# The first batch's attention input made inside the second batch's mixer stages instead of in a stage of its own

## The reference

```
x = _layernorm(x + _L0_attn_ref(x, ...))   # mixer: RMS norm, projections, convolution, state scan, gate
x = _layernorm(x + _L0_ffn_ref(x, ...))    # 4-bit block quantisation, 128x128 product
x = _layernorm(x + _L1_attn_ref(x, ...))   # attention, 16 heads of 64
x = _layernorm(x + _L1_ffn_ref(x, ...))    # experts: 8 routed, top 2, and a shared one
```

```
mu = jnp.mean(latents, axis=-1, keepdims=True)
var = jnp.mean((latents - mu) ** 2, axis=-1, keepdims=True)
x = (latents - mu) * jax.lax.rsqrt(var + 1e-05) * ln_gamma + ln_beta
q = (x @ Wq)...; k = (x @ Wk)...; v = (x @ Wv)...
```

## Time and profile before

| | us |
|---|---|
| median of 3 runs | 3421.25 |
| lowest and highest | 3419.8, 3422.25 |
| the profiled execution | 3422.55 |
| its span in the profile | 3420.8 |

### The profile page before, as it was taken

The page is one execution under the profiler, slowest core; times in us unless marked ns, Lnnn a source line. Parts: engine busy times, 40 slices in busy tenths (PEclk is TensorE's granted clock), DMA queues, the critical chain, the costliest instruction groups (busy, mean ns, idle before and its releaser), DMA issues. The chain is left out here.

```text
span 3420.8 us, 57281 instructions
## 1 busy us (share of the span) xinstructions
PE 3228.0 (94%) x20859; PEld 1947.6 (57%) x20861; DVE 2327.9 (68%) x3746; ACT 1999.1 (58%) x3828; POOL 2707.2 (79%) x1342
## 2 busy tenths in 40 slices
PE   6995899399999999999999999999999999998998
PEld 2554455155555555555555555555555555554898
DVE  3887688666667666666666776666676666664664
ACT  6984797245555555555655665555555555554454
POOL 1881386079999999999999999999999999996333
PEclk9997899699999999999999999999999999999999
DMA  2220121210000000000000000000000000000000
GB/s 51 91 87 21 53 89 59 59 28 1 4 1 4 4 1 4 1 4 1 4 1 4 7 7 7 1 4 1 4 1 4 4 1 2 1 1 22 20 24 12
DMA packets 66053, 59.95 MB, mean 18 GB/s; under 512 B 7786, under 2 KB 49332, under 8 KB 65716
## 3 DMA queue, kind: packets, MB, share of 16 engines
q1 hardware_dynamic: 63970, 55.93, 5.6%
q10 hardware_dynamic: 1810, 0.37, 0.1%
HBM read 49.46 MB, written 6.82 MB: 16 GB/s over the span
## 5 line engine op out<-in xcount | busy, mean ns | idle before, releaser
L1610 POOL TENSOR_TENSOR den_g<-den_g,p 128x1024 f32<-128x1024 f32 x888 | 2116.7, 2384 | 142.7 <-ACT p L1532 24.9
L1685 DVE TENSOR_REDUCE quarters<-psum 128x1 f32<-128x512 f32 x2004 | 1291.4, 686 | 648.8 <-PE psum L1061 604.4
L1532 ACT ACTIVATE p<-psum 128x512 f32<-128x512 f32 x2048 | 1084.4, 600 | 384.8 <-PE psum L1409 337.1
L1422 PE MATMUL psum<-p,v 128*64 128x512 f32 x4096 | 922.8, 592 | 0.0
L1422 PEld LDWEIGHTS psum<-p,v 128*64 128x64 f32 x4096 | 293.3, 137 | 582.0 <-issue 506.9
L1061 PE MATMUL psum<-k_main,q_main 64*128 64x512 f32 x2048 | 449.4, 424 | 6.9 <-DVE quarters L1068 5.6
L652 POOL TENSOR_TENSOR fed_s<-dx,work 128x1024 f32<-128x1024 f32 x128 | 302.2, 2363 | 179.2 <-POOLq L593 160.6
L1409 PE MATMUL psum<-row_shift,row_ones 64*128 64x512 f32 x2048 | 415.8, 389 | 0.0
L1409 PE MATMUL psum<-q_main,k_main 64*128 64x512 f32 x2048 | 413.4, 391 | 2.2 <-PEq L1201 2.2
L1409 PE MATMUL psum<-q_main,k_rest 64*128 64x512 f32 x2048 | 415.1, 390 | 0.0
L1409 PE MATMUL psum<-q_rest,k_main 64*128 64x512 f32 x2048 | 414.7, 390 | 0.0
(11 more groups left out here) (284 smaller groups left out, 3233.3 us busy)
## 6 DMA issues: line engine op xcount, KB each, us to landing
work<-bc_rows SPq DMA_DIRECT2D x128, 256.0 KB, 3.1
resid<-in_resid SPq DMA_DIRECT2D x8, 256.0 KB, 4.2
x_mid<-resid SPq DMA_DIRECT2D x8, 256.0 KB, 2.6
residual<-x_mid SPq DMA_DIRECT2D x8, 256.0 KB, 4.7
x<-x_mid SPq DMA_DIRECT2D x8, 256.0 KB, 2.8
out<-mixed SPq DMA_DIRECT2D x8, 256.0 KB, 2.3
xa<-x_mid SPq DMA_DIRECT2D x4, 256.0 KB, 3.6
w_qkv<-in_Wq SPq DMA_DIRECT2D x16, 64.0 KB, 1.9
```

Source lines behind the costliest of these rows:

```text
L1422: last = nc.tensor.matmul(o_bank[hi(h), :], vv[:, kt, hi(h)], p[:, u % LIVE, h, :], start=(kt == 0), stop=(kt == KT - 1))
L1532: nc.scalar.activation(p[:, u % LIVE, h, :], bank_of["score", u, h], ACT.Exp, scale=float(DH) ** -0.5).then_inc(p_ready, 1)
L1610: nc.gpsimd.tensor_tensor(sums, first, src, ALU.add).then_inc(added_g, 1)
L1685: nc.vector.reduce_max(quarters[:, to % 2, h, n:n + 1], bank_of["max", u, h], X_AXIS).then_inc(max_read, 1)
```

## The change

The block `attention_input` goes. Its steps are made from `resids[0]`, the mixer's buffer, while the second batch's mixer runs:

- in the second batch's `mixer_inputs`, VectorE makes the 16 statistics and aggregates behind its passes over PSUM, and GpSimd makes roots and offsets (`norm_roots`, with the power on GpSimd) into `stat_in`, which gets a fourth row;
- in the second batch's `mixer_output`, ScalarE scales the 16 tiles into `scaled_in` behind its half of the first norm, TensorE turns them into banks 4 to 7 behind the bias products, and ScalarE writes them to `xaT0` with gamma and beta. TensorE waits for `in_taken` before it turns the quantised values into the same banks. SP loads gamma, beta and the six weights of the first pairs at the head of this block;
- `xaT0`, `gamma`, `beta` and `w_qkv` are allocated ahead of phase 1; `xaT` becomes a list of two tiles;
- the set-up block has no DMA any more, and Wo's two loads go to the head of SP's queue in `attention_first`.

The diff, cut to its core:

```diff
+def norm_roots(nc, pool, st, two, stat, exponents, ready):
+    var, y, t, offset = (stat[:, i, :] for i in range(4))
+    pool.wait_ge(ready, TILES)
+    st.link(nc.gpsimd.tensor_scalar(var, two[:, :, 1], EPS, None, ALU.add))
+    st.link(nc.gpsimd.tensor_tensor(y, var, exponents, ALU.pow))
+    st.link(nc.gpsimd.tensor_tensor(t, y, y, ALU.mult))
+    st.link(nc.gpsimd.tensor_tensor(t, t, var, ALU.mult))
+    st.link(nc.gpsimd.tensor_scalar(t, t, -0.5, 1.5, ALU.mult, ALU.add))
+    st.link(nc.gpsimd.tensor_tensor(y, y, t, ALU.mult))
+    st.link(nc.gpsimd.tensor_tensor(offset, two[:, :, 0], y, ALU.mult))
+    return nc.gpsimd.tensor_scalar(offset, offset, -1.0, None, ALU.mult)
...
# mixer_inputs
+        else:
+            @block.gpsimd
+            def _(pool):
+                st = Steps(pool, pool_step)
+                norm_roots(nc, pool, st, two, stat_in, exponents[:], averaged).then_inc(roots, 1)
+                pool.wait_ge(roots, 1)
...
+            if following is None:
+                for t in range(TILES):
+                    nc.vector.bn_stats(six[:, t, :], resids[0][:, t, :]).then_inc(measured, 1)
+                dve.wait_ge(measured, TILES)
+                for t in range(TILES):
+                    nc.vector.bn_aggr(two[:, t, :], six[:, t, :]).then_inc(averaged, 1)
...
# mixer_output, TensorE
+                if last_batch:
+                    turn_input(nc, pe, psum, 4, scaled_in, ident, in_scaled, in_turned)
                 pe.wait_ge(quantised, 1)
                 for c in range(CHUNKS):
-                    if b + 1 < BATCH:
-                        pe.wait_ge(in_taken, c + 1)
+                    pe.wait_ge(in_taken, c + 1)
...
# mixer_output, SyncE
+                if last_batch:
+                    sp.dma_start(gamma[:], ins["ln_gamma"]).then_inc(weights, 16)
+                    sp.dma_start(beta[:], ins["ln_beta"]).then_inc(weights, 16)
+                    for pair in range(2):
+                        for i, w in enumerate(("Wq", "Wk", "Wv")):
+                            sp.dma_start(w_qkv[:, pair, i, :], ins[w][:, pair * P:(pair + 1) * P]).then_inc(weights, 16)
...
# mixer_output, ScalarE
+                    if turn == 1 and last_batch:
+                        for t in range(TILES):
+                            nc.scalar.activation(scaled_in[:, t, :], resids[0][:, t, :], ACT.Identity, scale=stat_in[:, 1, t:t + 1],
+                                                 bias=stat_in[:, 3, t:t + 1]).then_inc(in_scaled, 1)
+                        act.wait_ge(weights, 16 * 8)
+                        for c in range(CHUNKS):
+                            act.wait_ge(in_turned, c + 1)
+                            nc.scalar.activation(xaT0[:, piece(c)], banks(psum, 4 + c), ACT.Identity, scale=gamma[:, 0:1],
+                                                 bias=beta[:, 0:1]).then_inc(in_taken, 1)
...
# phase2
-                @block.sync
-                def _(sp):
-                    sp.dma_start(gamma[:], ins["ln_gamma"]).then_inc(loaded, 16)
-                    sp.dma_start(beta[:], ins["ln_beta"]).then_inc(loaded, 16)
-                    sp.wait_ge(loaded, 32)
...
-        attention_input(nc, ins, x_in, 0, common)
-        attention_first(nc, 0, common, experts)
+        attention_first(nc, ins, 0, common, experts)
...
# attention_first, SyncE
+                    for pair in range(2):
+                        sp.dma_start(w_o[:, pair, :], ins["Wo"][pair * P:(pair + 1) * P, :]).then_inc(w_o_loaded, 16)
                     for dst, src in experts["loads"]:
                         sp.dma_start(dst, src).then_inc(experts["loaded"], 16)
+                    sp.wait_ge(w_o_loaded, 32)
```

More of the change, by code:

```diff
@@ L214, in build @@
         shared = dict(ident=ident, ident_bf=ident_bf, ones=ones, exponent=exponent, psum=psum)
-        phase1(nc, ins, x_mid[0], **shared)
+        first = dict(xaT0=ph.sbuf("xaT0", [P, SEQ]), gamma=ph.sbuf("gamma", [P, 1]), beta=ph.sbuf("beta", [P, 1]),
+                     w_qkv=ph.sbuf("w_qkv", [P, 2, 3, P]))
+        phase1(nc, ins, x_mid[0], first, **shared)
         with Phase(nc) as late:
@@ L218, in build @@
             tail = attention_tail(late)
-            phase2(nc, ins, x_mid[0], x_mid[1], experts, tail, **shared)
+            phase2(nc, ins, x_mid[0], x_mid[1], experts, tail, first, **shared)
             phase3(nc, ins, x_mid[0], x_mid[1], out, experts, tail, **shared)
@@ L450, in mixer_inputs @@
         big = su.sbuf("big", [P, len(units), PIECE])
-        loaded, step, pool_step, squares, roots, in_scaled = (
-            su.sem(s) for s in "loaded step pool_step squares roots in_scaled".split())
+        loaded, step, pool_step, squares, roots, in_scaled, measured, averaged = (
+            su.sem(s) for s in "loaded step pool_step squares roots in_scaled measured averaged".split())
         conv_psum, conv_done, in_psum, tapped, tap_silu, skip_psum, skip_done = (
@@ L800, in mixer_scan, with mixer_output @@
         nc.all_engine_barrier(sems_to_clear=sem_range(su.sems))
-def mixer_output(nc, x_out, b, m):
+def mixer_output(nc, ins, x_out, b, m):
     resid, work, xnT, scaled_in, norm_w, ident, stat, gain_act, ffn_parts, bias_parts, ones_bf, psum, ident_bf, six, two = (
         m[k] for k in "resid work xnT scaled_in norm_w ident stat gain_act ffn_parts bias_parts ones_bf psum ident_bf six two".split())
+    resids, stat_in = m["resids"], m["stat_in"]
+    xaT0, gamma, beta, w_qkv = (m["first"][k] for k in "xaT0 gamma beta w_qkv".split())
+    last_batch = b + 1 == BATCH
     with Phase(nc, f"_o{b}") as su:
@@ L896, in attention_tail, with phase2 @@
         residual=ph.sbuf("residual", [P, CHUNKS, TPC, D]))
-def phase2(nc, ins, x_in, x_out, experts, tail, ident, ident_bf, ones, exponent, psum):
+def phase2(nc, ins, x_in, x_out, experts, tail, first, ident, ident_bf, ones, exponent, psum):
     with Phase(nc) as ph:
[L903 to L909, removed]
+        gamma, beta, w_qkv = (first[k] for k in "gamma beta w_qkv".split())
+        xaT = [first["xaT0"], ph.sbuf("xaT1", [P, SEQ])]
         v = ph.sbuf("v", [P, 2, TILES, P])
@@ L924, in phase2 @@
         shift = ph.sbuf("shift", [P, 2 * TPC, 64], BF16)
-        common = {k: x for k, x in locals().items() if k not in ("nc", "x_in", "x_out", "ins", "ph", "experts", "tail")}
+        common = {k: x for k, x in locals().items() if k not in ("nc", "x_in", "x_out", "ins", "ph", "experts", "tail", "first")}
         common.update(tail)
@@ L1275, in attention_pairs @@
     o_raw, den_g, den_v, rec, residual = (m[k] for k in "o_raw den_g den_v rec residual".split())
-    stat, gamma, beta, ident = (m[k] for k in "stat gamma beta ident".split())
+    gamma, beta, ident = (m[k] for k in "gamma beta ident".split())
     assert BATCH == 2
@@ L1455, in use @@
                             pe.wait_ge(weights, 48 * (g // CHUNKS))
-                        last = project(nc, bank, w, xaT[:, batch_of(g + CHUNKS)], projection(what, g))
+                        last = project(nc, bank, w, xaT[batch_of(g + CHUNKS)], projection(what, g))
                     last.then_inc(use_full, 1)
@@ L1495, in read_use @@
                     elif what == "input":
[L1496 removed]
+                        nc.scalar.activation(xaT[1][:, piece(g)], bank, ACT.Identity, scale=gamma[:, 0:1], bias=beta[:, 0:1]).then_inc(freed_by_scalar, 1)
                     elif what == "output":
```

68 lines of the change are left out of this document (13 added, 55 removed).

## The result

The changed kernel takes 3404.1 us, median of 5 runs (3402.55 to 3405.81), against 3421.43 for the kernel before (5 runs, 3419.8 to 3424.6). The ratio is 0.9947, with a 95% interval of 0.9934 to 0.9961. That is 17.3 us less, where 18.7 were forecast; 3404.1 lies inside the range of 3398.1 to 3407.4. Beside later experiments the same kernel ran again (a0_after) and was 19.05 us under the kernel before.

A forecast was written before the change was run, and what follows sets the result against it. Blocks add up between all-engine barriers, each as long as its slowest chain; no engine bounds the removed stage. Terms -19.95 + 0.5 + 0.7 = -18.7 us from 3421.25 give 3402.5 us, range 3398.1 to 3407.4.

The forecast's parts named there:

- The removed stage: At the border to attention_first: its matmuls begin at 645.47 in place of 665.42, 19.95 us less.
- The 0.98: Behind attention_input: time from the last copy to attention_first's first matmul, taken as the price of a barrier, 0.98 us.
- The moved work in mixer_inputs and mixer_output: In the second batch's mixer stages: the added work fits into idle time of the engines and costs nothing.
- The forecast's 7.5 us: In the second batch's mixer_output: TensorE's cover before it is needed at 623.42, about 7.5 us.
- Rival B: In mixer_output: work moved beside the quantisation slows it, costing 9.4 us, 3411.9 us in all; chance 0.03.
- The clock in attention_first: At the five projections: TensorE comes cold and runs 4.3 us at 1.2 GHz instead of 3.3, +0.5 us.
- Rival A: In attention_first: the clock stays low throughout, the gain falls to about 5.5 us, 3415.7 us; chance 0.03.
- The loop's start: At the attention loop's start: 4.3 us at the lower clock instead of 3.0, +0.7 us.
- Rival C: In the attention loop: tiles elsewhere in SBUF lengthen operand streams, 1.2% costs 29.3 us, 3431.8 us; chance 0.02.
- Rival D: At the border to attention_first: something the 19.5 us covered is late instead, time about 3420 us; chance 0.02.

The follow-up runs named there:

- x6_nopool: The changed kernel with GpSimd's two clears moved from the set-up block to the head of attention_first, VectorE's fills left; 3402.45 us in a single run.
- x1_added_only: The kernel before plus the work added to the second batch's mixer stages, with attention_input and the set-up block's two loads kept; 3421.03 us against 3421.66.
- the x3 pair: The changed kernel with ScalarE's 16 scalings of the first batch made twice or three times; 3402.01 and 3406.47 us in single runs.
- x2_warm: The changed kernel plus 52 useless matmuls at the end of the second batch's mixer_output and 16 useless transposes in the set-up block; 3400.5 us.

## Why the prediction was right, and where it was off

**The removed stage.** Forecast 19.95 us, or 19.6 if something other than SP's loads made the 1.33 us behind the fills. Measured 19.62. The step that failed is "The fills are late next, so attention_first should begin its matmuls at 644.49 + 0.98". That the loads came last was read rightly (beta landed 0.53 us behind the last fill), but without them the first projection still comes 1.32 us behind the fills. The 0.98 was taken from another border, and a border's cost isn't fixed: to the next block's first matmul it was 0.98 and 1.27 us behind attention_input, and 1.00, 1.22 and 1.74 ahead of the loop, by kernel. x6_nopool shows that it wasn't GpSimd's clear; the cause stays open.

**The moved work in mixer_inputs and mixer_output** was free, as forecast. VectorE had 11.92 us of cover left for 14 forecast, because in this profile TensorE's product came 16.2 us after the passes (352.10 to 368.32) and not 18.7: the granted clock stayed at 1.00 there, where the kernel before had 3.4 us at the lower level (361.6 to 365.0). In a0_after, whose clock fell there too, 14.36 us were left. The reads of PSUM were done at 615.8 for "near 616". x1_added_only shows that the whole of it costs nothing by itself, and the x3 pair that TensorE's cover is between 6.25 and 12.5 us. The forecast's 7.5 us was too thin, because it counted from the last read; it is 10 us. Rival B (wide passes slowed) falls by L170's unchanged 2.29 us and the unchanged start of the quantised transposes.

**The clock in attention_first.** Forecast +0.5, from 4.3 us at the lower clock, with ends at -0.2 and +2.7. Measured +1.23 to the first maxima, with 5.9 us there for 3.4. The mechanism and the price per us are shown by x2_warm and the table; the size varies by execution. The seven profiles without transposes and without filler had 2.7 to 5.9 us, mean 4.1, and took 7.84 us to the first maxima on average, 0.35 more than the kernel before. So +0.5 was somewhat over the mean effect and less than half of this profile's. (The lengths in the prediction were read from rows that end 0.1 to 0.2 us ahead of the rise; this changes no term.) The sentence of the Trainium skill, page "TensorE: Matmul & The Clock Gate", Part 1, that activity releases the throttle, agrees with x2_warm. It agrees with x1_added_only too, where the clock rose at 659.2, while the transposes were ending, but there it fell again at 662.6, 1.0 us into the projections. As a rule against this change it weighed little: with the transposes the projections had 3.4 us at the lower clock, without them 4.1 on average. Rival A (low through the whole of attention_first) appeared in no profile.

**The loop's start.** Forecast +0.7, measured +0.68, with 4.3 us at the lower clock for 3.1. That it hit so well is luck: a0_after had 6.1 there and x6_nopool 2.8.

**What was not in the sum.** What differs from execution to execution ahead of the change, the course of the granted clock in both scans above all. The forecast added 1.5 us for such things, from the spread of three runs. In the profile after they add up to +0.92 us against the profile before, in a0_after to -2.76. With the 0.33 at the border and the 0.73 of clock in attention_first, the 0.92 make the 2.0 us between the 18.7 forecast and the 16.74 of the two profiled executions. With a0_after's median the gain is 19.05, with the first 17.3; 18.7 lies between. That it is this near to both is partly luck, since the scatter is as large as the two terms that were too favourable.

**Rival C** (the loop slower by 1% from other places in SBUF): the loop took 2443.62 us before, 2444.30 and 2445.52 after, under 0.1%. **Rival D** fell by the result.

## What to carry to other kernels

A stage between two barriers is worth its full length if its work fits into idle time that other stages have anyway; find that time per engine, and follow the moved chain to the first wait of the host stage that it could delay. Behind a stage that goes, look at once at what the border still waits for: here the set-up block (3.2 us, of which 0.2 came back at the next border) and a store whose result nobody needs yet (2.4 us) were worth another 5.3 us by the medians. When TensorE comes cold to a short dense stage, count half of the time that it spends at the lower clock, and read that time in several profiles, since it differs from execution to execution.

## What the runs showed of the hardware

- The clock took one of two courses through the same scan. The second batch's had two falls more in three of 13 profiles, and was 2.1 to 3.2 us longer there; the first batch's was 205.33 us in one and 207.55 to 208.23 in twelve. Two profiles of one kernel were 3.7 us apart ahead of the first changed stage (600.83 and 597.15).
- TensorE work without use paid: 11.39 us of it in a wait, with 16 transposes in the set-up block, took 1.33 us off the path to the first maxima against a0_after (7.13 to 5.80) and 2.92 against the first profile of the same kernel (8.72).
- A us of the projections at 1.2 GHz cost 0.49 to 0.50 us of the path, in nine profiles with 2.7 to 5.9 us of it.
- From the last work of a block over the barrier of all engines to the next block's first matmul it took 0.98, 1.27 or 1.32 us ahead of attention_first where VectorE came last (before, x1_added_only, after). Ahead of the loop it took 1.00 to 1.03 us in seven profiles with the set-up block, 1.22 or 1.23 in the five without it, and 1.74 in x1_added_only. The cause is open.
- VectorE's two fills of row_shift took 0.98 us beside GpSimd's clear of shift and 0.76 in x6_nopool without it. GpSimd's power over 128x16 values took 2.93 us (2.91 in the earlier trace rows), more than its seven other operations together.
